# A mixture-of-experts kernel: the weights of experts 1 to 3 are loaded after the first token lists instead of at the attention's end

## The reference

```
x  : 16 x 128 x 512 = 2048 tokens of 512, float32
x = x + cross_attention(layernorm(x), ctx, ...)       # 16 heads, 16 key tiles
x = x + moe(layernorm(x)):
      scores = softmax(h @ gate_w.T)                  # 16 experts
      top 6 experts of each token, weights = scores
      y = sum over chosen e: w_e * (silu(h @ w_gate[e].T) * (h @ w_up[e].T)) @ w_down[e].T   # inner size 352
x = x + memory_attention(layernorm(x), ctx, mask)
x = x + gated_mlp(h) + product_key_experts(h)         # 512 -> 2048 -> 512, top 8 of 1024
```

## Time and profile before

| | |
|---|---|
| median of 3 runs | 1928.22 us (1927.49, 1928.22, 1937.55) |
| the profiled execution's own time | 1926.74 us |
| its span | 1925.0 us |
| TensorE matmuls busy | 1801.6 us, 94% of the span |
| DVE, ACT, POOL busy | 1093.7, 884.7, 820.2 us |
| mean granted TensorE clock | 0.977 |
| moved by SP's queue | 157.47 MB |
| moved by GpSimd's queue | 126.29 MB |

### The profile page before, as it was taken

One profiled execution on the slowest core, in us unless ns is written; L12 is line 12 of the kernel. 1 busy time (PEld: TensorE's weight loads), 2 busy tenths in 40 slices (PEclk: granted clock), 3 DMA queues, 4 the chain that ended last, 5 costly groups with the idle time before them and its releaser, 6 DMA issues.

```text
span 1925.0 us, 39526 instructions
## 1 busy us (share of the span) xinstructions
PE 1801.6 (94%) x12786; PEld 1073.8 (56%) x12789; DVE 1093.7 (57%) x2985; ACT 884.7 (46%) x1833; POOL 820.2 (43%) x731
## 2 busy tenths in 40 slices
PE   6989999999972999999999999995899999999998
PEld 3566666766631666666666666663554444444444
DVE  4578888888852323322322323223656877777776
ACT  4588888888841443444434434433732221122111
POOL 4234456656664344443433443442112444544442
PEclk9999999999985999999999999998999999999999
DMA  8255587777776666766665765545012355555653
GB/s 310 88 163 175 178 164 168 186 178 170 182 161 166 159 147 145 160 163 152 146 150 135 165 153 100 93 82 129 33 35 66 125 187 202 206 171 210 203 178 143
DMA packets 137921, 294.81 MB, mean 153 GB/s; under 512 B 39200, under 2 KB 64416, under 8 KB 133600
## 3 DMA queue, kind: packets, MB, share of 16 engines
q1 hardware_dynamic: 86752, 157.47, 29.5%
q0 software_dynamic: 46368, 126.29, 26.7%
q10 hardware_dynamic: 4608, 8.52, 1.5%
HBM read 426.00 MB, written 78.33 MB: 262 GB/s over the span
## 4 chain that ended last, share of the span: by engine, by line
PE 81%; DVE 6%; DMA 4%; issue 4%; ACT 3%; POOL 1%; SPq 0%; another core or an unknown queue 0%; ACTq 0%; POOLq 0%; DVEq 0%
PE bank L234 21%; PE bank L236 21%; PE bank L235 21%; PE bank L1061 3%; PE bank L1088 2%; PE bank L851 1%; DVE work_arena L1578 1%; DMA x_sum<-x,work_arena 1%; PE bank L927 1%; ACT xt_arena L1314 1%; PE bank L842 1%; POOL expert_tokens L2226 1%; DMA work_arena<-in_ctxT 1%; DMA work_arena<-in_pk_w 1%; DMA work_arena<-in_moe_w 1%
## 5 line engine op out<-in xcount | busy, mean ns | idle before, releaser
L234 PE MATMUL bank<-work_arena,xt_arena 128*128 x1221 | 404.7, 331 | 2.8 <-DVE xt_arena L2072 1.9
L235 PE MATMUL bank<-work_arena,xt_arena 128*128 x1221 | 404.6, 331 | 0.0
L236 PE MATMUL bank<-work_arena,xt_arena 128*128 x1221 | 404.5, 331 | 0.0
L2311 POOL DMA_INDIRECT x_sum<-x,work_arena x111 | 176.5, 1590 | 392.5 <-DMA x_sum<-x,work_arena 222.9
L2060 DVE TENSOR_TENSOR xt_arena<-xt_arena,bank 128x352 f32<-128x352 f32 x111 | 57.9, 522 | 405.9 <-PE bank L236 373.0
L234 PE MATMUL bank<-work_arena 128*128 128x512 f16 (+1 forms) x600 | 226.3, 378 | 15.1 <-DVE x L1883 6.8
L235 PE MATMUL bank<-work_arena 128*128 128x512 f16 (+1 forms) x600 | 226.4, 379 | 0.0
L236 PE MATMUL bank<-work_arena 128*128 128x512 f16 (+1 forms) x600 | 226.3, 378 | 0.0
L1468 ACT ACTIVATE xt_arena<-bank 128x1024 f16<-128x1024 f16 x111 | 113.6, 1023 | 224.4 <-PE bank L1061 212.0
L234 PE MATMUL bank<-xt_arena,work_arena 128*128 128x512 f16 x528 | 200.1, 379 | 1.7 <-DVE xt_arena L194 1.7
L235 PE MATMUL bank<-xt_arena,work_arena 128*128 128x512 f16 x528 | 200.1, 379 | 0.0
(11 more groups left out here) (278 smaller groups left out, 3823.0 us busy)
## 6 DMA issues: line engine op xcount, KB each, us to landing
work_arena<-expert_w SPq DMA_DIRECT2D x111, 1408.0 KB
work_arena<-expert_w SPq DMA_DIRECT2D x111, 768.0 KB
work_arena<-in_moe_w SPq DMA_DIRECT2D x64, 352.0 KB
expert_w<-work_arena SPq DMA_DIRECT2D x64, 352.0 KB
work_arena<-in_moe_w SPq DMA_DIRECT2D x64, 192.0 KB
expert_w<-xt_arena SPq DMA_DIRECT2D x64, 192.0 KB
work_arena<-in_mlp_w SPq DMA_DIRECT2D x8, 1536.0 KB
work_arena<-in_head_w SPq DMA_DIRECT2D x16, 512.0 KB, 5.6
```

Source lines behind the costliest of these rows:

```text
L234: pe.matmul(o, a_hi, b_hi, start=start, stop=False)
L235: pe.matmul(o, a_hi, b_lo, start=False, stop=False)
L236: return pe.matmul(o, a_lo, b_hi, start=False, stop=stop)
L2311: pool.indirect_dma_start(out=xacc[:, :], out_offset=bass.IndirectOffsetOnAxis(ap=rid[:, i:i + 1], axis=0), in_=ysb[:, b % YB, :], in_offs ...
```

## The change

Only the order of SP's program is changed. At the attention's end just expert 0's two loads are issued. The loads of experts 1 to 3 come after the first list, one part between that list and lists 1 to 3, two parts between these and lists 4 to 7, and the rest behind them. The wait for `y_mm` on SP goes away. The same bytes are loaded to the same places, with the same semaphores.

```diff
             sp.wait_ge(q_mm, q_at["heads", NT - 1, 3] + 1)
             first_a(0)
-            for e in range(SLOTS - 1):
-                first_d(e)
-            sp.wait_ge(y_mm, STEPS)
-            first_a(1)
+            first_d(0)
...
             sp.wait_ge(placed, 16 * TOPE * NT)
             sp.dma_start(rid[:, 0:1], recs[0:P, :]).then_inc(first_list, 16)
+            first_a(1)
             records(0)
+            first_d(1)
+            first_a(2)
             records(1)
-            first_a(2)
+            first_d(2)
+            first_a(3)
             first_d(3)
-            first_a(3)
             held = {}
```

## The result

| | before | changed |
|---|---|---|
| median of 20 runs each | 1931.13 us (1924.28 to 1938.24) | 1935.95 us (1931.78 to 1944.92) |
| ratio changed / before | | 1.0028, 95% interval 1.0014 to 1.0041 |
| profiled execution, span | 1925.0 us | 1933.6 us |

The change makes the kernel slower by 0.28%: 0.0028 x 1931.13 = 5.4 us, interval 2.7 to 7.9. That lies within the 0.5% that I called no change, but it is clear of zero, and I had forecast zero. (The two medians alone give 1.0025.) The time came out where the slower rival had put it (5.0 to 7.4 us over), though only in small part for that rival's reason.

The account below looks back on a forecast made before the run. TensorE bounds 81% of the span, but transfers set the handover from attention to experts. Drain -5.0 plus lists 1.7 and gather 3.3 sum to 0.0 us, so 1928.2 us; range 1922 to 1935.

Parts of the forecast that it names:

- slower rival: At the drain, scatters set its end themselves: nothing gained, the start costs 5.0 to 7.4 us; chance 0.2.
- drain (M1): Last list scatter's issue to first list's issue: removing 3.0 MB of early weights saves 5.0 us (bounds 0 and 6.4).
- lists (G): T (first list's issue) to block 1's gather: 1408 KB ahead of lists 1 to 3 adds 1.7 us (0.4 to 2.5).
- gather of block 1 and what follows (M2 - G): Block 1's gather issue to first expert matmul: the gather running beside weight loads adds 3.3 us (0 to 4.9).
- The handover as the only place: Between attention and experts: the one place the edit touches where TensorE has nothing to do, so transfers can matter.
- The instructions' cost: One more issue between first list and lists 1 to 3 costs about 0.4 us; later moved loads cost nothing.
- no weight load comes late: After the first expert matmul: TensorE waits for no weight load; slack 7 us, no cost.
- at most: In the drain: an indirect store without weights lands in 4.78 us, so the gain is 6.4 us at most.
- the first list at 604 or later: Sign in the changed trace: first list issued at 604 us or later means the slower rival holds.
- later than 601 us: Deciding mark: first list issued later than 601 us means the drain's gain is less than the start's loss.
- The clock: TensorE's clock, returning after about 4 us of expert matmuls: priced at nothing; half of any shift is won or lost.
- faster rival: At the start, gathers aren't held up by weights: net -1.6 to -4.3 us, time 1924 to 1926.6; chance 0.23.

Follow-up runs that it names:

- e7: e2 with ten of the last eleven list scatters left out; last scatter's issue to first list's issue took 8.04 us.
- e13: Changed kernel, but SP waits until the first list has landed before issuing expert 1's gate/up weights; first list's issue to first expert matmul 18.19 us.
- e9: The kernel before, unchanged, executed again; last scatter's issue to first list's issue 7.59 us, to first expert matmul 19.55 us.
- e1: Changed kernel with expert 1's gate/up weights moved behind lists 1 to 3; ratio to before 1.0001 (0.9979 to 1.0023).
- e8: Changed kernel with expert 1's gate/up weights issued by ScalarE on ACT's queue; first list's issue to block 1's gather issue 10.16 us.
- e5: Changed kernel, but expert 1's gate/up weights issued at the attention's end, all else of experts 1 to 3 behind lists 1 to 7; ratio to before 0.9997.
- e11: Kernel before with down loads of experts 1 and 2 still early, expert 1's gate/up weights behind lists 4 to 7; last scatter to first list 7.60 us.
- e16: Same kernel as e5, timed once more; ratio to before 0.9998 (0.9984 to 1.0012).
- e2: Changed kernel with all loads of experts 1 to 3 behind lists 1 to 7; ratio to before 0.9996 (0.9977 to 1.0016).
- e4: Kernel before with 3.0 MB of early weights issued between SP's waits for stored rows and for scatters, the rest as before; ratio 1.0021 (0.9998 to 1.0043).

## Why the prediction was wrong

The sum had three terms. Means of four executions before and two of the changed kernel:

| term | predicted | measured |
|---|---|---|
| drain (M1) | -5.0 (bounds 0, -6.4) | 10.40 to 7.83: -2.6 (from the last product on: -1.5) |
| lists (G) | +1.7 (bounds 0.4, 2.5) | 6.36 to 10.60: +4.2 |
| gather of block 1 and what follows (M2 - G) | +3.3 (bounds 0, 4.9) | 4.87 to 8.86: +4.0 |
| sum | 0.0 | +5.65 (timed: +5.4) |

- The handover as the only place, the chain that sets it, and that nothing else moves: right (behind the first expert matmul 1307.2 to 1312.3 us are left in four executions before, 1308.1 and 1308.0 in the changed kernel). The instructions' cost (a few tenths) was right, and so was that no weight load comes late.
- Lists: the step that failed most, and the only one beyond its own bounds. "List 3 would be there at T + 6.35 by itself ... and lands 0 to 1.5 us behind the weights' end" treated it as a matter of place in the queue and of the weights' full rate from T + 2.1 on. The weights hardly moved at first (32 GB/s from 604 to 610) and their first 1.44 MB were through at T + 7.6 instead of T + 5.5 to 6.9; list 3 came 2.8 us behind that, not 0 to 1.5. And the sum held nothing for the list ahead of them, which came at 6.1 us instead of 2.1 to 3.6: in the first pair of traces that alone moves block 1's gather by 3.1 us. No row of before shows a load directly behind a list; the nearest was in the earlier trace rows, where weights kept a gather at 1 packet for 2.1 us, and I used it for the gather only.
- Drain: the step failed in the bound "at most". I took 4.78 us, the landing of another kind of indirect store, for an unhindered scatter; it is 8 us (e7). From a drain of 11.25 that leaves 3.2 to gain, not 6.4, and the earlier trace rows weighed packets that had been handed over, not writes that had landed. And the 11.25 of one execution is not the kernel's: it runs from 7.6 to 13.1.
- Gather: right in kind, and 4.0 against 3.3 in size. That it was priced at two thirds because it "is first in its queue" was an argument without a row. The rule of the Trainium skill ("DMA: Bandwidth & Descriptors", "Queues, rings and completion order": a completion lands only after the engine's earlier writes) had spoken for nearer 4.9; the trace agrees with its direction (8.15 us against 3.15). The first list, 6.1 us in the changed kernel against 3.0 in e13, was delayed by weights issued behind it, which earlier writes don't explain.
- The slower rival had the time (5.0 to 7.4 over) by another way: a drain that gains nothing plus a start of +5. In fact the drain gains 1.5 to 2.6 and the start costs 8.2. That the scatters end the drain by themselves is so in the changed kernel and in e9, but it is the 8 us of the last one, with the engines idle, and not writes that hold up the engines. Its sign by which to know it, the first list at 604 or later, was met (605.79), but only since that execution's attention ended later; a place in the span was the wrong sign, a difference from the last scatter would have been the right one. For the same reason its "later than 601 us" could not be judged.
- The clock was priced at nothing, with half of a shift to be won or lost. By windows of 0.25 us it is back at its upper level (2.4 GHz, 1.00) 3.6 to 4.6 us after the first expert matmul in the four executions before, 2.1 and 1.9 us after it in the changed kernel. A product takes 0.29 us at the lower level and 0.15 at the upper, so this gave back about 1 us: 8.2 - 1.0 less the 1.5 to 2.6 is 4.6 to 5.7 (my estimate), the timed loss 5.4.
- The faster rival (queues taking turns packet by packet) is refuted for the lists and the gather by e1 and e8: in a queue of its own the small transfer is not quicker.
- A slip of reading without consequence: the 89% busy engines of the earlier trace rows belong to 588 to 596, where TensorE still had 0.50 us of work, and not to its idle time from 596 on.
- The range ended at 1935.0. Over the 1928.22 I started from, the ratio gives 1933.6 (1930.9 to 1936.1); the 20 runs have before at 1931.13 and the changed kernel at 1935.95. So the range was missed by the start from three runs as much as by the sum; it also ended 0.6 under the slower rival's own upper end, 1935.6. That the handover would come out even is what failed.

## What to carry to other kernels

Where a wait ends a stage, find out what part of it a transfer needs by itself before pricing what traffic costs it: here 8 of 11 us were fixed. Short transfers that release the next stage (index lists, first rows) should have the DMA engines for themselves; a bulk load put right behind the first of them delays it too. In this kernel half of the 3 MB at the attention's end left M1 at 7.6 to 8.5 us (e5, e11, e16), against 7.6 to 8.3 with none. And measure a stretch from two ends: the same edit gains 2.6 us from the last scatter on and 1.5 from the attention's end on.

## What was not expected of the hardware

- A scatter of 128 words of 4 bytes to HBM needs 7.5 to 8.2 us from its issue to its landing with idle DMA engines, the same alone or as the last of eleven (M1 8.04 in e7 against 8.08 in e2); no packet is recorded in the last 6 of them (591 to 597.5 us in e7). A list load of 0.5 KB needs 2.0 to 3.6 us with no weights under way (before, e9).
- A load issued 0.4 us behind such a list delays it to 6.1 us (e13: 3.0 with the load held back), from another queue too (e8, where the gather of block 0 starts 5.8 us after the list's issue).
- Weights issued beside the last scatters move at 54 GB/s in their first 4 us with the engines 80% busy (e4), and the last scatter takes 14.7 us instead of about 8.
- The same load, issued 3.0 us after a list instead of 0.4, moves 1.0 MB in three us instead of 0.16 (e13 against the changed kernel, from 1.0 and 0.6 us behind its issue).
- One program's handover (M1 + M2) varies from 19.6 to 24.3 us between executions, and the last scatter's issue lies at 585.4 us of the span in e2 and at 597.8 in the changed kernel, which are the same program up to there.
